# Differential attention: the planner of the stage gets another price for each change of TensorE's tiling, and no delay between TensorE's own steps

## The reference, cut to what matters

```python
        q = rope_rotate(q).reshape(b, s, H, 2, D)
        k = rope_rotate(k).reshape(b, s, H, 2, D)
        q1, q2 = (q[..., 0, :], q[..., 1, :])
        k1, k2 = (k[..., 0, :], k[..., 1, :])
...
        o1 = sdpa(q1, k1, vfull)
        o2 = sdpa(q2, k2, vfull)
        o = o1 - lam * o2
        ms = jnp.mean(jnp.square(o), axis=-1, keepdims=True)
        o = o * jax.lax.rsqrt(ms + EPS) * ln_w + ln_b
        o = o * (1.0 - LAMBDA_INIT)
        o = o.reshape(b, s, e)
        return o @ Wo.T
```

## Time and profile before

| what | us |
|---|---|
| median of 3 runs | 2881.08 (2879.59 to 2883.12) |
| profiled execution, span from first to last instruction | 2876.6 |
| of it before stage c's planned part (to the first `c_s`) | 510.8 |
| stage c from its first `c_s` to its last `c_ft` | 1027.8 |
| what follows | 1338.0 |
| TensorE busy | 2806.9 |
| VectorE busy | 2168.8 |
| ScalarE busy | 1650.4 |

### The profile page before, as it was taken

The page is one execution under the profiler, slowest core; times in us unless marked ns, Lnnn a source line. Parts: engine busy times, 40 slices in busy tenths (PEclk is TensorE's granted clock), DMA queues, the critical chain, the costliest instruction groups (busy, mean ns, idle before and its releaser), DMA issues.

```text
span 2876.6 us, 52549 instructions
## 1 busy us (share of the span) xinstructions
PE 2806.9 (98%) x20384; PEld 1887.3 (66%) x20384; DVE 2168.8 (75%) x5059; ACT 1650.4 (57%) x3488; POOL 1055.4 (37%) x1210
## 2 busy tenths in 40 slices
PE   8999999999999999999998899999999999999998
PEld 7777877333333333333335788888888888888887
DVE  7885545788788778877874777777777778888886
ACT  3222332665565656566664676666666766666663
POOL 5343442024113311421322444444445554544442
PEclk9999999999999999999999999999999999999999
DMA  2000010320321222042202100000000100000001
GB/s 80 23 10 23 8 23 3 41 29 11 41 24 18 27 30 28 7 58 24 32 16 76 29 5 5 4 5 5 11 20 26 33 27 5 12 12 12 11 12 61
DMA packets 49149, 66.65 MB, mean 23 GB/s; under 512 B 12590, under 2 KB 37124, under 8 KB 48900
## 3 DMA queue, kind: packets, MB, share of 16 engines
q1 hardware_dynamic: 48900, 63.29, 12.4%
HBM read 24.99 MB, written 8.39 MB: 12 GB/s over the span
## 4 chain that ended last, share of the span: by engine, by line
PE 89%; DVE 5%; ACT 3%; DMA 1%; POOL 1%; issue 1%; SPq 0%; POOLq 0%; ACTq 0%; DVEq 0%
PE ps L1416 17%; PE pw L220 17%; PE ps L220 13%; PE pw L1403 11%; PE ps L1202 6%; PE pw L1202 5%; PE ps L1576 4%; PE pw L1527 3%; PE pw L1489 2%; PE pw L1509 2%; PE ps L1489 1%; PE pw L1352 1%; PE ps L1527 1%; DMA c_qst<-c_mr 1%; PE ps L1386 1%
## 5 line engine op out<-in xcount | busy, mean ns | idle before, releaser
L1707 ACT ACTIVATE c_p<-pw 128x512 f32<-128x512 f32 x1024 | 562.2, 595 | 337.6 <-PE ps L1386 179.7
L1416 PE MATMUL ps<-c_p,c_vals 128*64 128x512 f32 x2048 | 547.7, 618 | 2.9 <-ACT c_p L1707 1.6
L1995 DVE TENSOR_REDUCE c_mx<-ps 128x1 f32<-128x512 f32 x694 | 462.7, 683 | 111.8 <-PE ps L1386 103.6
L1403 PEld LDWEIGHTS pw<-c_qst,c_kst 50*128 50x128 f32 x1024 | 154.8, 185 | 366.3 <-ACT c_p L1707 271.8
L1403 PE MATMUL pw<-c_qst,c_kst 50*128 50x512 f32 x1024 | 384.6, 450 | 7.5 <-DMA c_qst<-c_mr 6.6
L1386 PE MATMUL ps<-c_kst,c_qst 48*128 48x512 f32 x694 | 289.5, 453 | 1.5 <-DVE c_mx L1995 0.8
L1761 ACT ACTIVATE e_sm<-e_sm,e_mx 128x256 f32<-128x256 f32 x512 | 254.0, 500 | 63.5 <-DVE e_mx L2140 63.3
L1995 DVE TENSOR_REDUCE c_mx<-pw 128x1 f32<-128x512 f32 x330 | 225.5, 683 | 45.7 <-PE pw L1386 42.2
L2363 POOL TENSOR_TENSOR e_ss<-e_ss,half 128x16 f32<-128x16 f32 x64 | 186.7, 2917 | 118.4 <-DVE e_ss L2097 104.6
L2260 POOL TENSOR_SCALAR stat<-stat 128x1 f32<-128x1 f32 (+1 forms) x141 | 33.7, 239 | 522.2 <-DVE stat L1867 464.0
L1416 PEld LDWEIGHTS ps<-c_p,c_vals 128*64 128x64 f32 x2048 | 104.3, 135 | 181.6 <-issue 161.3
(11 more groups left out here) (316 smaller groups left out, 6355.6 us busy)
## 6 DMA issues: line engine op xcount, KB each, us to landing
c_kst<-shared SPq DMA_DIRECT2D x192, 64.0 KB
c_qst<-shared SPq DMA_DIRECT2D x64, 128.0 KB
x<-in_L_attn_x SPq DMA_DIRECT2D x8, 512.0 KB, 3.9
c_qst<-shared SPq DMA_DIRECT2D x64, 64.0 KB
keep<-x SPq DMA_DIRECT2D x8, 512.0 KB, 4.0
e_raw<-keep SPq DMA_DIRECT2D x8, 512.0 KB, 3.5
e_hs<-x SPq DMA_DIRECT2D x64, 63.0 KB
out<-x SPq DMA_DIRECT2D x7, 512.0 KB, 5.1
```

The costliest lines, as they stand in the source:

```text
L1403: e.matmul(bank_of("c_s", n, sh, kt, h), c_kst[i][p0:p0 + 50, sh // 2, 128 * kt:128 * kt + 128], c_qst[i][p0:p0 + 50, sh // 2, 512 * h:512 ...
L1416: ins = e.matmul(pv[64 * h:64 * h + 64, :], c_v[:, kt, 33 * hd:33 * hd + 64], p[:, 512 * h:512 * h + 512], start=kt == 0, stop=kt == 7, sk ...
L1707: e.activation(c_p[slot["c_p", (n, sh, kt)]][:, 512 * h:512 * h + 512], bank_of("c_s", n, sh, kt, h), ACT.Exp, scale=0.5).then_inc(SC, 1)
L1995: e.tensor_reduce(c_mx[m % 2][:, qt, h:h + 1], bank_of("c_max", n, sh, qt, h), AX.X, ALU.max).then_inc(VE, 1)
```

## The change

It alters the planner's numbers for stage c, and two rules of the planner: a step of an engine no longer waits the lag after an earlier step of the same engine (`own=True`), and the lag after a step can depend on its kind. No instruction is added, removed or altered; stages a, b and d keep their order.

```diff
-        "pe c_s": 0.34, "act c_s": 0.6, "dve c_max": 0.67, "dve c_mm": 0.16, "pe c_row": 0.12, "act c_row": 0.26,
-        "dve c_row": 0.27, "sp row_in": 2.5, "sp c_stack": 5.9, "pe c_w": 0.92, "act c_o": 0.56, "pe c_ft": 0.46,
+        "pe c_s": 0.23, "act c_s": 0.6, "dve c_max": 0.67, "dve c_mm": 0.16, "pe c_row": 0.1, "act c_row": 0.26,
+        "dve c_row": 0.27, "sp row_in": 2.5, "sp c_stack": 5.9, "pe c_w": 0.86, "act c_o": 0.56, "pe c_ft": 0.44,
...
-PACE, NEAR = 16.73, 0.16
-DUE_C = {"pe c_s": -2.7, "act c_s": 13.5, "dve c_max": 12.3, "dve c_mm": -8.4, "c_row": -19.7, "row_in": -24.9,
+PACE, NEAR, TURNS = 16.7993, 0.0863, 0.177
+DUE_C = {"pe c_s": -0.9, "act c_s": 40.9, "dve c_max": 12.1, "dve c_mm": -127.7, "c_row": -122.8, "row_in": -46.9,
...
-        return self.over_at.get((e, k, v), 0.0) + self.lags.get(e, self.lag)
+        return self.over_at.get((e, k, v), 0.0) + self.lags.get((e, k), self.lags.get(e, self.lag))
...
-            o["from"] = max([self.after(*r) for r in o["refs"]] or [0.0])
+            o["from"] = max([self.over_at.get(r, 0.0) if self.own and r[0] == o["eng"] else self.after(*r) for r in o["refs"]] or [0.0])
...
-            order = Order(P, NEAR, {"pe": 0.22}, 0.06, 0.09)
+            lags = {"pe": 0.21, ("pe", "c_s"): 0.31, ("pe", "c_w"): 0.42, ("pe", "c_two"): 0.42}
+            order = Order(P, NEAR, lags, 0.06, TURNS, own=True)
```

More of the change, by code:

```diff
@@ L49 @@
        "dve n_nm": 48.7, "d_x": -0.2}
-PACE, NEAR = 16.73, 0.16
-DUE_C = {"pe c_s": -2.7, "act c_s": 13.5, "dve c_max": 12.3, "dve c_mm": -8.4, "c_row": -19.7, "row_in": -24.9,
-         "c_stack": -4.2, "pe c_w": 4.4, "act c_o": 21, "pe c_ft": -11.4, "dve c_ft": -18.8, "pool c_ft": 27.2,
-         "c_n": -28.1, "c_val": -1, "c_x": -1.2, "c_rot": 143.7, "pool c_sum": 129.1, "pool c_part": 132.4,
-         "c_ot": 8, "c_wo": 40.4, "n_c": 19.5}
+PACE, NEAR, TURNS = 16.7993, 0.0863, 0.177
+DUE_C = {"pe c_s": -0.9, "act c_s": 40.9, "dve c_max": 12.1, "dve c_mm": -127.7, "c_row": -122.8, "row_in": -46.9,
+         "c_stack": 10.3, "pe c_w": 3.8, "act c_o": -60.7, "pe c_ft": -55.5, "dve c_ft": 18, "pool c_ft": -10.7,
+         "c_n": -117, "c_val": -5, "c_x": -5.9, "c_rot": 222.8, "pool c_sum": 264.4, "pool c_part": 126.9,
+         "c_ot": 32.4, "c_wo": 32.7, "n_c": 67.1}
 PACE_A, NEAR_A = 8.4, 0.06
@@ L135, with __init__ @@
 class Order:
-    def __init__(self, plan, eps, lags, lag, turn=0.0):
-        self.P, self.eps, self.lags, self.lag, self.turn = plan, eps, lags, lag, turn
+    def __init__(self, plan, eps, lags, lag, turn=0.0, own=False):
+        self.P, self.eps, self.lags, self.lag, self.turn, self.own = plan, eps, lags, lag, turn, own
         self.over_at, self.engine_at, self.blocked, self.ready, self.mode = {}, Counter(), {}, [], None
     def after(self, e, k, v):
-        return self.over_at.get((e, k, v), 0.0) + self.lags.get(e, self.lag)
+        return self.over_at.get((e, k, v), 0.0) + self.lags.get((e, k), self.lags.get(e, self.lag))
     def room_at(self, item):
```

## The result

The changed kernel takes 2829.29 us (median of 4 runs, 2827.32 to 2830.15), the kernel before beside it on the same chip 2882.1 us (4 runs, 2879.59 to 2883.48). The ratio is 0.9817, 95% interval [0.9805, 0.9828]: 1.8% faster, 52.8 us between the medians. The profiled span goes from 2876.6 to 2825.5 us, 51.1 less. The forecast was 2837.9 us, 43.2 less than before.

A forecast was written before the change was run, and what follows sets the result against it. TensorE was taken as the bound in stage c. Fewer tiling changes, -58.2 us, exp waits, +12.8, and bank waits, +2.2, gave -43.2: 2837.9 us, forecast range 2828 to 2856, wider range 2824 to 2862.

The forecast's parts named there:

- the price of a round: TensorE in stage c: entering and leaving both tilings, pairs and weightings, costs 0.346 us, 0.173 for each change.
- The term of -58.2 us: Stage c: fewer pair groups (536 to 403) and weighting groups (481 to 267) save 25.9 and 32.3 us.
- the quiet map: Map with only its own steps: group prices sum to 14.25 against 14.28 us measured before; 14.0 forecast after.
- `WW`: Two weightings in a row; behind three pairs the second starts at 1.80 us, its exp ends at 1.63, no wait.
- Waits of a lone `c_w` for its exp: Stage c: 44 weightings close behind their `c_s` wait 0.29 us each for the exp, +12.8 us.
- Waits for banks: Pairs in stage c wait for one of three banks per ring; only +2.2 us, with `c_o` between exps.
- the form `PPPrfPP`: Three pairs, `c_row`, `c_ft`, two pairs, in 11 maps: the second pair's bank comes 0.2 us late, +2.2 us.
- its own entry from pairs, 0.11 more: Quiet map before: pairs ahead of `c_ft` last 0.77 in place of 0.66 us, taken as a price of tiling.
- I leave the 6.6 us as they are: TensorE's waits in stage c for the DMA that brings the row maxima: 6.6 us, expected unchanged.
- The new waits take most: Rival: waits at banks after groups of three leave a gain of 6 to 25 us, 2856 to 2875; chance 0.17.
- VectorE and the three banks: Rival: each group of three waits for the group before's maximum; slower, 2899 at 0.3 us each; chance 0.06.
- Nothing that can be measured: Rival: the round's price is local or paid as waits elsewhere; within 0.2%, 5.8 us; chance 0.06.

The follow-up runs named there:

- tiny_whole: Changed kernel with an eight-column product on all TensorE rows ahead of each `c_s` directly behind a pair, 600 places, adding two tiling changes each; 3049.08 us.
- short_copy: Kernel before, with the copy `c_o` over 256 of its 512 columns from the second map on; 2879.11 us, ratio 0.999.
- half_max: Changed kernel with each VectorE maximum taken over 256 of its 512 columns; 2826.84 us, ratio 0.9808.
- old_due: Changed kernel with the due times, PACE and NEAR of the kernel before; 2877.23 us, ratio interval 0.9975 to 0.9994.
- half_exp: Changed kernel with each exp from the second map on taken over 256 of its 512 columns; 2821.98 us, ratio 0.9796.
- turn_alone: Kernel before, with only the planner's price for a change of tiling raised from 0.09 to 0.177; 2933.66 us, ratio 1.0183.
- turn_zero: Changed kernel with the planner's price for a change of tiling set to zero; 2962.79 us, ratio 1.0285.
- own_alone: Kernel before, with only the rule that a step does not wait the lag after a step of its own engine; 2867.2 us, ratio 0.9951.
- recalibrated: Changed planner with durations and delays taken from the traces, and due times to go with them; 2821.33 us, ratio 0.9796.
- tiny_pair: Changed kernel with the same 600 eight-column products, but on the rows of the pair's own half, adding no tiling change; 2881.3 us.

## Why the prediction was right, and where it was off

- **What bounds, and the price of a round.** Right. In the whole stage groups of three last 0.895 us (the median of 139 ahead of a step on the whole array), double weightings 1.867 (95), triple ones 2.725 (35), single ones 1.009 (84), single pairs 0.43 (59). The term of -58.2 us stands. That a change of tiling has a price is shown by tiny_whole, at 0.145 us for another pair of tilings. The prediction's own test, the quiet map at 14.25 for 14.28, was weaker than it looks: its `c_row` was taken from what was left (the trace bears the 0.20 out: 0.203, the median of 62), and its 0.11 at `c_ft` was a wait. A slip without effect: the second weighting of a `WW` starts at 0.89 + 0.86 = 1.75, not 1.80, still behind its exp.
- **Waits of a lone `c_w` for its exp.** Right: forecast 44 times 0.29, 12.8 us; measured 43 places and 12.5 us. Of these 39, with 11.3 us, are a lone weighting behind three pairs; two, with 1.1, stand at the start of the stage, where before has the like. The quiet map came out at 13.98 us for 14.0.
- **Waits for banks.** Forecast 2.2 us. Measured 7.5 us at 21 places where an exp holds the bank and 1.6 at 23 where a maximum does, 9.1 in all (before 1.3). The step looked only at the `c_o` in the form `PPPrfPP`, and that came out: 10 maps, 0.19 us each at the second pair, for 11 at 0.2. It had nothing for a fourth pair. Nine groups of four last 1.67 us in place of 1.13, 4.9 us in all, the largest part of what was missing. So this term is 7.8 - 2.2 = 5.6 us too small, in the direction of slower.
- **The entry of `c_ft`.** The step "its own entry from pairs, 0.11 more" failed: short_copy shows a wait for the copy there. Before, 99 groups of two pairs ahead of whole-array steps averaged 0.752 us against 0.661, 9.0 us in all; after, such waits are 2.8 us. With `c_o` directly behind `c_row` and three pairs ahead of `c_ft`, the copy is over nearly in time (31 places still wait 0.07): 6.2 us that the sum did not have.
- **The row's DMA.** "I leave the 6.6 us as they are" was mis-sized: 1.0 us is left, 5.6 less. The first weighting of the stage waits 2.8 us, now for `c_xb`, where 1.4 was its share before.
- **The sum again.** -58.2 + 12.5 + 7.8 - 6.2 - 5.6 + 1.4 = -48.3 us, against -50.7 in the stage. The 2.4 us lie in small waits that the list leaves out or, as at the start of the stage, counts as new: over all groups of pairs and weightings, what they last beyond their price is 30.8 us before and 38.2 after, 7.4 more and not 9.9, and -58.2 + 7.4 = -50.8 is what the stage shows.
- **Luck.** The gain of 52.8 us stands at the very end of the forecast's 25 to 53. The range held because the misses partly cancel: 7 us of new waits that the sum did not have, against 11.8 us of old ones that went. The prediction expected none of the old ones to go.
- **The rivals.** "The new waits take most" did not happen: new waits are about 22 us and 12 of old ones went. "VectorE and the three banks" did not either (half_max), but old_due shows how near it was. With the same groups' sum and pairs beyond the third of their group the gain is all but gone. The prediction asked whether groups of three would wait for the group before them; the place where three banks bite is the fourth pair, and the third one as soon as the wait for the exp is gone (half_exp). "Nothing that can be measured" fell with the price of the tiling. Ways to fail by waits of the row's DMA or a fallen clock are real, in turn_alone and turn_zero, not in this order.

## What to carry to other kernels

Where an engine shows 97% busy, measure from start to start: a change of tiling can hide inside the matmuls' busy time, and the number of changes times its price, which two groups of different length give, forecasts what a reordering can give at best. Of the seven orders here that sum was within 5 us of the measured difference from before in three (changed, own_alone, recalibrated), and in the other four the kernel was 37 to 77 us slower than it says. It is only a floor: check besides that no run of steps is longer than its ring of buffers, and that loads a map ahead still come in time. A planner's prices, delays and due times belong together, and changing one without the others cost up to 81 us against the kernel before.

## What was not expected of the hardware

- Consecutive passes overlap in the records: an exp over 512 columns lasts 0.595 us but follows the one before at 0.49, a maximum lasts 0.683 and follows at 0.61.
- Half the columns do not take half the time: 0.381 us for an exp and 0.414 for a maximum over 256.
- 1200 more changes between pairs and the whole array cost 0.145 us each where nothing waits (tiny_whole against tiny_pair), less than the 0.173, on average, between pairs and weightings.
- In turn_zero the granted clock was at the 1.2 GHz level (0.51 to 0.53) over 21 to 28 us around waits of up to 23.5 us.
